# Two-layer adaLN transformer on one core: another layout in DRAM for the three-part queries and keys, a pace of its own for batch 0, and a later wait for the setup's stores

## The reference

```python
# layer 0
h = layernorm(x) * (1 + ca) + sa
x = x + ga * (light_attention(h) + routed_heavy_attention(h))   # 8 heads of 64, window 64; 256 routed queries and keys
h = layernorm(x) * (1 + cb) + sb
x = x + gb * ffn_per_channel(h)                                 # 64 channels, 16 inner units each
# layer 1
h = layernorm(x) * (1 + ca) + sa
x = x + ga * causal_attention(h)                                # 16 heads of 16, q and k normalised, rope
h = layernorm(x) * (1 + cb) + sb
x = x + gb * (gelu(h @ sign(w1) * alpha1 + b1) @ sign(w2) * alpha2 + b2)
```

## Time and profile before

| | |
|---|---|
| median of the runs, us | 4387.87 |
| profiled execution, its time | 4394.76 |
| profiled execution, its span | 4393.0 |
| mean granted TensorE clock | 0.901 |
| TensorE (PE) busy | 3662.8 us, 83% of the span |
| VectorE (DVE) busy | 2511.7 us, 57% |
| ScalarE (ACT) busy | 1934.2 us, 44% |
| GpSimd (POOL) busy | 1486.2 us, 34% |
| SyncE's stores of parts | 576 (384 to `split_q`, 192 to `split_k`), 64 KB each |
| SyncE's loads of parts | 64 of q, 192 of k |

### The profile page before, as it was taken

The page is one execution under the profiler, slowest core; times in us unless marked ns, Lnnn a source line. Parts: engine busy times, 40 slices in busy tenths (PEclk is TensorE's granted clock), DMA queues, the critical chain, the costliest instruction groups (busy, mean ns, idle before and its releaser), DMA issues. The chain is left out here.

```text
span 4393.0 us, 59749 instructions
## 1 busy us (share of the span) xinstructions
PE 3662.8 (83%) x19241; PEld 2053.7 (47%) x19241; DVE 2511.7 (57%) x6732; ACT 1934.2 (44%) x4521; POOL 1486.2 (34%) x1807
## 2 busy tenths in 40 slices
PE   6378569987799878997799887998799887998787
PEld 2245334464446534464445544465344654465433
DVE  6754547357563666547573665636574565736652
ACT  5134334544264443554355442644435443544433
POOL 4133342244323441234412433234412444134311
PEclk8589789998899988998899988998899988999788
DMA  6110231002300022002300023002210023000120
GB/s 229 67 32 13 48 77 31 14 15 48 93 13 23 24 60 69 18 12 50 88 20 13 22 44 90 15 22 44 67 45 14 12 52 93 13 24 22 42 58 6
DMA packets 207650, 191.30 MB, mean 44 GB/s; under 512 B 12993, under 2 KB 189377, under 8 KB 207306
## 3 DMA queue, kind: packets, MB, share of 16 engines
q1 hardware_dynamic: 203298, 177.94, 16.0%
q0 software_dynamic: 3328, 8.39, 0.7%
q10 hardware_dynamic: 720, 1.15, 0.1%
HBM read 121.73 MB, written 65.11 MB: 43 GB/s over the span
## 5 line engine op out<-in xcount | busy, mean ns | idle before, releaser
L2322 ACT ACTIVATE arena<-pb 128x512 f32<-128x512 f32 (+3 forms) x1536 | 670.9, 491 | 338.9 <-PE pb L1557 333.1
L2402 POOL TENSOR_TENSOR arena<-arena,small 128x512 f32<-128x512 f32 x256 | 284.7, 1116 | 481.8 <-DVE small L1732 481.4
L2151 ACT ACTIVATE arena<-arena,small 128x256 f32<-128x256 f32 x512 | 256.0, 500 | 416.9 <-DVE small L1715 416.3
L2566 POOL TENSOR_SCALAR_AFFINE_SELECT arena<-arena 128x256 f32<-128x256 f32 x512 | 219.5, 432 | 603.0 <-ACT arena L2322 601.7
L1574 PE MATMUL pb<-arena,v 128*17 128x512 f32 (+3 forms) x3072 | 368.1, 512 | 28.4 <-POOL arena L2566 19.7
L2006 DVE TENSOR_REDUCE arena<-pb 128x1 f32<-128x512 f32 x512 | 333.1, 682 | 97.6 <-PE pb L1532 96.4
L1557 PE MATMUL pb<-arena 98*128 98x512 bf16 (+3 forms) x1152 | 355.0, 344 | 11.3 <-ACT arena L2322 6.6
L1715 DVE CUSTOM_DVE_ANT_0 arena<-pb,wmask 128x256 f32<-128x256 f32 x512 | 196.0, 420 | 237.8 <-PE pb L1274 237.8
L1998 DVE TENSOR_REDUCE arena<-pb 128x4 f32<-128x512 f32 x256 | 173.0, 688 | 232.1 <-PE pb L1523 229.9
L1274 PE MATMUL pb<-arena 128*128 128x256 f32 x1024 | 285.8, 405 | 5.2 <-issue 4.5
L1652 PE MATMUL pb<-xh,w1T 128*128 128x512 f32 x512 | 267.0, 662 | 10.0 <-DVE xh L1872 8.6
(11 more groups left out here) (354 smaller groups left out, 7597.4 us busy)
## 6 DMA issues: line engine op xcount, KB each, us to landing
split_q<-arena SPq DMA_DIRECT2D x384, 64.0 KB
arena<-split_q SPq DMA_DIRECT2D x64, 384.0 KB, 5.4
split_k<-arena SPq DMA_DIRECT2D x192, 64.0 KB
arena<-split_k SPq DMA_DIRECT2D x24, 384.0 KB, 6.4
xn<-h_d SPq DMA_DIRECT2D x8, 1024.0 KB, 11.7
xt<-in_x SPq DMA_DIRECT2D x16, 512.0 KB, 3.9
heavy_d<-arena SPq DMA_DIRECT2D x8, 1024.0 KB, 4.4
xn<-heavy_d SPq DMA_DIRECT2D x8, 1024.0 KB, 5.5
```

The costliest lines, as they stand in the source:

```text
L2151: ins = s.activation(pm[n % 3][:, j], sm[n % 2][:, j], ACT.Exp, bias=nmx[:, 2 * sl + j:2 * sl + j + 1], scale=-1.0, accum_out=sml[:, 2 * s ...
L2322: s.activation(pp[pn % 4][:, h % 2, 0:w_], bank[n % 3][:, 0:w_], ACT.Exp).then_inc(a_exp1, 1)
L2402: g.tensor_tensor(pm[n % 3], pm[n % 3], rcl[:, 2 * sl:2 * sl + 2].unsqueeze(2).broadcast_to([P, 2, 2 * P]), ALU.mult).then_inc(p_norm0, 1)
L2566: g.affine_select(out=p2, in_=p2, pattern=[[0, 2], [1, P]], compare_op=ALU.is_ge, fill=0.0, base=0, channel_multiplier=-1).then_inc(p_tri, 1)
```

## The change

Seven edits.

1. `split_q` and `split_k` both become (16 heads, 16 columns, 6 rows, 1024): the column comes ahead of the row, and k has all six rows in DRAM, too. A DRAM row of a store for tile row (h, d) then lies at a constant pitch over all 128 rows.
2. A chain issues 10 stores. `put_rows` writes one part to two or three rows at once, with a repeated (stride 0) source; `put` writes one `lo` part for both halves of the heads.
3. `load_group` issues one DMA for k.
4. `FIRST` replaces `PACE` for `light` in batch 0: (3.01, 0.54) for (1.88, 0.9) in its first half, (1.2, 1.1) for (1.0, 1.0) in its second. The first number is for the projections, the second for the attention steps.
5. For the last `u` of the setup, the move of `cs` goes ahead of the store of `h_d`.
6. The wait for the stores of `h_d` moves from the end of the setup block to the pick block, ahead of the load of `xn`; `r_h` is released with that block.
7. `two_valued` waits for the store of u = 5 before it writes its scratch.

```diff
+FIRST = {("light", 0): (3.01, 0.54), ("light", 1): (1.2, 1.1)}
 def pace_of(key, n, pace):
     if key[0] == "light":
-        return PACE[key[0], key[2]][n >= (17, 12)[key[2]]]
+        return (PACE if key[1] else FIRST)[key[0], key[2]][n >= (17, 12)[key[2]]]
-SPLIT_DMAS = 18
+SPLIT_DMAS = 10
-        split_q = dram("split_q", (H1, 6, HD1, N), BF16)
-        split_k = dram("split_k", (H1, 3, HD1, N), BF16)
+        split_q, split_k = (dram(n, (H1, HD1, 6, N), BF16) for n in ("split_q", "split_k"))
...
                 for u in range(B):
+                    if u + 1 == B:
+                        sp.wait_ge(r_row, 2 * (u + 1))
+                        sp.dma_start(cs[16 * u:16 * (u + 1), :], s_row).then_inc(r_cs, 16)
                     sp.wait_ge(r_add, u + 1)
                     sp.dma_start(h_d[u * N:(u + 1) * N, :]...)
-                    sp.wait_ge(r_row, 2 * (u + 1))
-                    sp.dma_start(cs[16 * u:16 * (u + 1), :], s_row).then_inc(r_cs, 16)
+                    if u + 1 < B:
+                        sp.wait_ge(r_row, 2 * (u + 1))
+                        sp.dma_start(cs[16 * u:16 * (u + 1), :], s_row).then_inc(r_cs, 16)
...
-                for i in range(XB):
-                    sp.wait_ge(r_h[i], 16 * (1 + (i + XB < B)))      # end of setup
...
+                for i in range(XB):
+                    sp.wait_ge(r_h[i], 16 * (1 + (i + XB < B)))      # pick block
                 sp.dma_start(xn[:, :, :], h_d[0:N, :]...)
...
                         if m >= 2:
                             v.wait_ge(b_add, m - 1)
+                        else:
+                            v.wait_ge(r_h[0], 16 * 2)
...
-                    sp.dma_start(qa[..][0:KS], split_q[heads, :, :, ..].rearrange("h r d n -> (r d) h n"))
-                    for r0, n in ((0, 3), (3, 2), (5, 1)):
-                        sp.dma_start(ka[..][r0 * HD1:(r0 + n) * HD1, ..], split_k[heads, 0:n, :, ..].rearrange("h r d n -> (r d) h n"))
+                    sp.dma_start(qa[..][0:KS], split_q[heads, :, :, ..].rearrange("h d r n -> (d r) h n"))
+                    sp.dma_start(ka[..][0:KS, ..], split_k[heads, :, :, ..].rearrange("h d r n -> (d r) h n"))
...
-                    def put(dst, rows_, i, m0):
-                        for row in rows_:
-                            for m in range(2):
-                                heads = slice(m * P // HD1, (m + 1) * P // HD1)
-                                sp.dma_start(dst[heads, row, :, x0 * P:(x0 + 2) * P], L.parts[i][:, m0 + m])
+                    def put(dst, row, i, m0):
+                        sp.dma_start(dst[:, :, row, x0 * P:(x0 + 2) * P].rearrange("(m h) d n -> (h d) m n", m=2), L.parts[i][:, m0:m0 + 2])
+                    def put_rows(dst, rows_, i, m0):
+                        n_rows = len(range(6)[rows_])
+                        for m in range(2):
+                            heads = slice(m * P // HD1, (m + 1) * P // HD1)
+                            sp.dma_start(dst[heads, :, rows_, x0 * P:(x0 + 2) * P].rearrange("h d r n -> (h d) r n"),
+                                         L.parts[i][:, m0 + m].unsqueeze(1).broadcast_to([P, n_rows, 2 * P]))
...
-                    put(split_q, (0, 1, 2), 0, 0)            # waits as before, in the same order
-                    put(split_q, (3, 4), 1, 0)
-                    put(split_k, (0,), 0, 2)
-                    put(split_q, (5,), 2, 0)
-                    put(split_k, (1,), 1, 2)
-                    put(split_k, (2,), 2, 2)
+                    put_rows(split_q, slice(0, 3), 0, 0)
+                    put_rows(split_q, slice(3, 6, 2), 1, 0)
+                    put_rows(split_k, slice(2, 5), 0, 2)
+                    put(split_q, 4, 2, 0)
+                    put_rows(split_k, slice(1, 6, 4), 1, 2)
+                    put(split_k, 0, 2, 2)
```

More of the change, by code:

```diff
@@ L213, in group_loaded @@
     before = sum(slot(*divmod(i, NG)) == slot(c, g) for i in range(NG * c + g + 1))
-    return 64 * (SLOT_LOADS[slot(c, g)] * b + before)
+    return 32 * (SLOT_LOADS[slot(c, g)] * b + before)
 def att_base(b, c, g):
@@ L380, in adaln_kernel @@
         XB = 5
-        r_x, r_h, r_mod = ([setup_sem(f"{n}{i}") for i in range(k)] for n, k in (("r_x", XB), ("r_h", XB), ("r_mod", 2)))
+        r_x, r_mod = ([setup_sem(f"{n}{i}") for i in range(k)] for n, k in (("r_x", XB), ("r_mod", 2)))
         r_stat, r_var, r_pow, r_nb, r_xhat, r_turn, r_hTa, r_hTv, r_dot, r_row, r_cs, r_mul, r_add = (
             setup_sem(n) for n in ("r_stat", "r_var", "r_pow", "r_nb", "r_xhat", "r_turn", "r_hTa", "r_hTv", "r_dot", "r_row", "r_cs", "r_mul", "r_add"))
+        r_h = [pick_sem(f"r_h{i}") for i in range(XB)]
         N_CONST = 7
@@ L2617, in load_group @@
                     landed = slot_in[slot(c, g)]
-                    sp.dma_start(qa[slot(c, g)][0:KS], split_q[heads, :, :, c * NH:(c + 1) * NH].rearrange("h r d n -> (r d) h n")).then_inc(landed, 16)
-                    for r0, n in ((0, 3), (3, 2), (5, 1)):
-                        sp.dma_start(ka[slot(c, g)][r0 * HD1:(r0 + n) * HD1, :, 0:(c + 1) * NH],
-                                     split_k[heads, 0:n, :, 0:(c + 1) * NH].rearrange("h r d n -> (r d) h n")).then_inc(landed, 16)
+                    sp.dma_start(qa[slot(c, g)][0:KS], split_q[heads, :, :, c * NH:(c + 1) * NH].rearrange("h d r n -> (d r) h n")).then_inc(landed, 16)
+                    sp.dma_start(ka[slot(c, g)][0:KS, :, 0:(c + 1) * NH],
+                                 split_k[heads, :, :, 0:(c + 1) * NH].rearrange("h d r n -> (d r) h n")).then_inc(landed, 16)
                 def put_row(b, c, g):
@@ L2673, in chain @@
                     n, L, x0 = 2 * b + c, lane[j], TH * c + 2 * j
-                    def put(dst, rows_, i, m0):
-                        for row in rows_:
-                            for m in range(2):
-                                heads = slice(m * P // HD1, (m + 1) * P // HD1)
-                                sp.dma_start(dst[heads, row, :, x0 * P:(x0 + 2) * P], L.parts[i][:, m0 + m]).then_inc(split_out[c][j], 16)
+                    def put(dst, row, i, m0):
+                        sp.dma_start(dst[:, :, row, x0 * P:(x0 + 2) * P].rearrange("(m h) d n -> (h d) m n", m=2), L.parts[i][:, m0:m0 + 2]).then_inc(split_out[c][j], 16)
+                    def put_rows(dst, rows_, i, m0):
[3 more added lines that the diff above has]
+                            sp.dma_start(dst[heads, :, rows_, x0 * P:(x0 + 2) * P].rearrange("h d r n -> (h d) r n"),
+                                         L.parts[i][:, m0 + m].unsqueeze(1).broadcast_to([P, n_rows, 2 * P])).then_inc(split_out[c][j], 16)
                     for _ in range(38):
```

## The result

The changed kernel takes 4311.1 us in the median of 4 runs (4302.0 to 4320.8), beside 4388.6 us for the kernel before on the same chip: a ratio of 0.983, 95% interval 0.981 to 0.985. Five more runs of it in another set gave 4303.2 us and 0.981 (0.979 to 0.983). Forecast were 4305 us, and faster. The profiled execution took 4313.04 us, 81.7 us less than that of before.

The account below looks back on a forecast made before the run. TensorE, the busiest engine, was taken to wait for key loads held up by SyncE's store issue; 36 + 5 + 22 + 17 + 4 = 84 us off 4394.8 gave 4311 profiled, 4305 as median, range 4284 to 4325 (0.62).

Parts of the forecast that it names:

- Term 1: Entry to the second half, batches 1 to 7: load goes out 4.3 us earlier, -36 us of an excess of 38.7.
- The price of a store: SyncE's issue of a new store taken as 0.45 us, between 0.38 for the nearest form and the old 0.6.
- rival of half the engines: Stores stay on 8 engines, so the load after the last `lo` part goes out 0.6 us later: 4353 us; chance 0.10.
- Rival of slow rows: Stored rows at a pitch of 12 KB write slowly, 87 ns a row: 4401 us; chance 0.05, of it 0.04 slower.
- Term 2: Entry to the first half, batches 1 to 7: two load issues fewer for the first group, -5 us, bounds 0 and 7.
- My factor of 0.7: First-half entry: 0.7 us a batch taken between 1.0 if issue sets the landing and 0 if the engines do.
- Term 3: Batch 0 up to its first fill: local attention covers nearly all of both chains, -22 us, between bounds of 2 and 32.
- this bound: Batch 0: at busy share 0.88 local attention ends at 471 and the fill starts at 479, a gain of 32.
- the other bound: Batch 0: each round costs 1.78 us, local attention ends at 498 and the fill comes at 509, a gain of 2.
- The first rival: Batch 0's pace gives nothing: 2 us up to the first fill, 10 from there to the transposes, 4331 us; chance 0.16.
- Term 4: Batch 0, first fill to the MLP's transposes: chains staggered by 9 rounds, -17 us, between bounds of 10 and 22.
- Term 5: Setup: `cs` ahead of the last `h_d` store lets the pick block's barrier fall at 109 to 110, -4 us.

Follow-up runs that it names:

- single_rows: Changed kernel with each row written by a store of its own, 24 stores a chain instead of 10, new DRAM order kept: 4336.3 us, ratio 0.987.
- k_three: Changed kernel with each group's load of keys in three DMAs again instead of one, same bytes: 4323.6 us, ratio 0.985.
- old_pace: Changed kernel with batch 0 back at the old pace; layout, stores, loads and setup stay changed: 4323.4 us, ratio 0.984.
- pace_only: Kernel before with only the new pace of batch 0 (`FIRST`) added: 4368.3 us, ratio 0.994.
- setup_old: Changed kernel with the setup as it was, `cs` behind the last `h_d` store and the barrier waiting for that store: 4313.1 us, ratio 0.983.
- pace_c: Changed kernel with the attention-step pace of batch 0's second half at 0.9 for 1.1: 4308.3 us, ratio 0.982.
- pairs_pace: Changed kernel with each batch's first group loaded in two pairs of heads and the second-half pace at 0.9: 4306.0 us, ratio 0.981.
- pairs_pace_mid: Like `pairs_pace`, but with batch 0's attention-step paces 0.58 and 1.0 for 0.54 and 0.9: 4292.1 us, ratio 0.978.
- head_pairs: Changed kernel with the first group of each batch loaded in two pairs of heads: 4299.9 us, ratio 0.980.

## Why the prediction was right, and where it wasn't

**Term 1 (-36): right.** Measured -39.0. The load goes out 3.1 us behind the last `lo` part, where I had 2.4: the last store's issue began 0.4 us behind the part, as the store ahead of it was still being issued, and its landing took 2.25 us (1100.36 + 0.49 = 1100.85 to 1103.10) for 1.76. So the load gained 3.6 us for the 4.3 I had, and that was enough all the same, as the excess is gone in all seven batches. `single_rows` shows the number of stores to matter: with 24 the excess is 23.5.

**The price of a store (0.45, nearest row 0.38).** Too low by a fifth: the last six stores of chain 3 take 0.49 to 0.53 us each, and with the gaps between them (1097.62 to 1100.85) 0.54. It did little harm, since only the last of them stands behind the last `lo` part. The number of stores, on which the sum of term 1 rests, is not the larger part of the gain: with 24 stores a chain the order in DRAM is worth 49 us and the merging 25 to 33. The prediction had the order only as a second look and as a rival. The share of 0.40 goes with eight engines at work, and the changed kernel's stores reach nine tenths. The rival of half the engines is out by the slices above.

**Rival of slow rows: out.** At 290 GB/s on 16 engines a row of 512 bytes takes 512 x 16 / 290 = 28 ns at the pitch of 12 KB, the 30 ns that I had from the pitch of 2 KB.

**Term 2 (-5): right, -6.9.** 1.0 us an entry. `k_three`, with two further issues, loses 1.2, which speaks for the issue, though its loads also differ in the engines that they seem to use. My factor of 0.7 for the share of 0.92 was not needed.

**Term 3 (-22): mis-sized, -10.5.** The step that failed is "the local attention ends at 471, and with the 8 us of the load the fill starts at 479": it puts nothing but the load behind the end of local attention. Local attention ended where this bound had it, within 3 to 8 us (478.5, and 473.9 in the second profile, for 471). (The 204 us of TensorE work on which the bound rests are at the clock of 0.95 of the first stretch, not at the full clock, as the prediction says; as the share of 0.88 is of that stretch, too, the 232 us stand.) But the chain's tail stood bare for 12.4 us to its last store, waiting on the way for engines in turn: its last `lo` parts began at 487.25 and 489.13 with 2.6 and 0.7 us of waits for ScalarE. The two bare rounds of the other bound, 3.6 us at 1.78 each, were these 12.4 us. Rounds of the order tell which instruction comes next, not how long a round lasts that holds only a dependent chain. `old_pace` shows how little the pace had to do with it: the first fill stays where it is when the pace is taken back. The first rival was right that the pace adds little at the first fill, but the shorter stores alone gave more there than its 2 us (263.3 us from the main block's start to the fill in `old_pace`, for 272.3). It was wrong behind the fill, where it left term 4 at 10 and 21.4 came.

**Term 4 (-17): mis-sized a little, -21.4**, nearly the upper bound of 22. The stores alone give 8.2 of it (`old_pace`) and the pace alone 20.7 (`pace_only`), so the pace has nearly all of it and the stores add less than 1 us to that.

**Term 5 (-4): the edit is worth 4.3 us at the start of the pick block and 3.5 at that of the main block** by `setup_old`. The two profiles of before and after show only 1.6 (main block) and 2.5 (pick block), since the setup itself ran 1.8 us later in the one of after (its last `h_d` store at 110.26 for 108.47). Over all profiles the main block starts at 236.4 us in the mean of ten with the edit, and at 239.8 in the mean of three without it.

**What the sum left out.** The terms measured make 79.4. The tail behind batch 7's third fill gave 5.5 more, which no edit reaches (it is told of below), and all else lost 3.2. That the total came within a few us of the forecast is in part luck: term 3 fell short by 11.5, and terms 1, 2 and 4 with the tail made up for it.

## What to carry to other kernels

When the DMA share stands at or below a half with a store always in flight, look at the slices of a tenth of a us and at the time of a packet. Here the share never stayed above 5 tenths while a packet took no longer than in the faster order, and another order of dimensions in DRAM lifted it to nine tenths. Shorten the last transfers ahead of a bare wait first; a microsecond there came back whole in each of seven batches. Don't price a stretch of an interleaved order by its count of rounds when one of its lanes is a dependent chain: the end of that chain can be the bound (in `old_pace` the other lane ended 27 us earlier and the fill didn't move), until the other lane ends later (in `pace_c`).

## What was unexpected

**The tail has two lengths.** From batch 7's third fill to the end of TensorE's last matmul it takes 177.4 to 178.3 us in seven of the 13 profiles and 182.0 to 184.3 in the other six, with the same instructions. No edit reaches it: `pairs_pace` has 184.26 and `pairs_pace_mid`, which differs in batch 0 alone, 177.48. Whether one kernel takes both lengths isn't shown; the only one profiled twice, the changed kernel, has the short one both times. The length goes with the granted clock of this stretch in all 13 profiles: 0.91 to 0.92 in the seven, 0.88 to 0.89 in the six. The windows of 20 us at 80 and 60 us ahead of the end differ in the granted clock, 0.83 and 0.69 in the first of the two, 1.00 and 0.86 in the second, that is more or less of the time at the lower of its two levels, 1.2 for 2.4 GHz (columns as in the earlier trace rows, `pairs_pace` and then `pairs_pace_mid`):

```profile
4221.30:4241.30 20.00, 17.96 (x89) 4.54 (x90) 0.68 (x2) 12.25 (x29) 2.80 (x7) 0.83 0.00 1
4241.30:4261.30 20.00, 10.95 (x44) 8.05 (x44) 6.43 (x20) 3.88 (x7) 7.07 (x8) 0.69 0.00 0
```
```profile
4214.80:4234.80 20.00, 16.95 (x102) 4.64 (x100) 1.37 (x3) 14.34 (x33) 3.22 (x8) 1.00 0.00 1
4234.80:4254.80 20.00, 10.52 (x61) 6.99 (x60) 6.43 (x20) 5.14 (x11) 8.17 (x10) 0.86 0.00 0
```

What tips it is not known. It is 4 to 7 us of a time in which I looked for gains of as much, so edits like `pace_c` and `head_pairs` are better judged by their own stretch than by the total.

**Gains in the same place don't add up.** In batch 0 up to the MLP's transposes 20 and 28 us of two edits alone gave 34 together. Behind the fill 8.2 and 20.7 us alone are 21.4 together, so there the pace had already removed nearly all that the stores could.
